# Two levels of attention scores from one product: six groups of queries over the same keys

## The reference, cut to what matters

```python
def step(S, inp):
    qt, kt, vt, gt = inp
    S = S * jnp.exp(gt)[..., None] + kt[..., None] * vt[..., None, :]
    o = jnp.einsum('bhk,bhkv->bhv', qt * scale, S)
    return (S, o)
...
f = 1.0 - k
sign_f = jnp.sign(f4 - 0.5)
theta = jnp.cumsum(sign_f, axis=1) * PI
```

## Time and profile before

| what | value |
|---|---|
| median of 3 runs | 1885.78 us (1882.69 to 1887.09) |
| profiled execution | 1883.84 us, its span 1881.9 us |
| TensorE busy | 1836.1 us, 98% of the span |
| VectorE busy | 1457.9 us, 77% |
| ScalarE busy | 696.8 us, 37% |
| GpSimd busy | 391.4 us, 21% |
| mean granted TensorE clock | 0.994 |
| first score product of block 1 and of block 31 | 107.47 and 1279.06 us |

### The profile page before, as it was taken

The page is one execution under the profiler, slowest core; times in us unless marked ns, Lnnn a source line. Parts: engine busy times, 40 slices in busy tenths (PEclk is TensorE's granted clock), DMA queues, the critical chain, the costliest instruction groups (busy, mean ns, idle before and its releaser), DMA issues. The chain is left out here.

```text
span 1881.9 us, 56458 instructions
## 1 busy us (share of the span) xinstructions
PE 1836.1 (98%) x24873; PEld 1648.7 (88%) x24873; DVE 1457.9 (77%) x2885; ACT 696.8 (37%) x1360; POOL 391.4 (21%) x309
## 2 busy tenths in 40 slices
PE   5899999999999999999999999998999999999999
PEld 5789998999989998899988999887888888888887
DVE  4577777677777777777777777778899889889886
ACT  2243334333343333333333333343334434433433
POOL 1001100111011100111001110012244444344343
PEclk9899999999999999999999999999999999999999
DMA  7010100001000010001100011002111111111110
GB/s 280 3 47 25 47 25 25 24 28 43 25 25 24 33 39 25 24 25 36 35 25 24 25 37 35 24 26 68 60 53 68 68 51 62 68 57 57 68 57 34
DMA packets 42650, 84.88 MB, mean 45 GB/s; under 512 B 2324, under 2 KB 2856, under 8 KB 42408
## 3 DMA queue, kind: packets, MB, share of 16 engines
q1 hardware_dynamic: 38552, 74.46, 11.3%
q10 hardware_dynamic: 3856, 6.82, 1.0%
HBM read 47.72 MB, written 33.55 MB: 43 GB/s over the span
## 5 line engine op out<-in xcount | busy, mean ns | idle before, releaser
L130 POOL TENSOR_TENSOR ln_rs<-ln_ve,mhalf 128x2 f32<-128x2 f32 x64 | 71.2, 1113 | 1011.1 <-DVE ln_ve L125 1011.1
L324 POOL TENSOR_TENSOR xs<-xs,y 128x512 f32<-128x512 f32 x64 | 83.5, 1305 | 368.3 <-DVE y L697 368.3
L1099 PE MATMUL bank<-hT_hi,wq_hi 128*128 128x256 f32 x512 | 152.5, 298 | 4.4 <-DVE wq_lo L1043 4.4
L1099 PE MATMUL bank<-hT_hi,wk_hi 128*128 128x256 f32 x512 | 151.4, 296 | 0.0
L730 DVE TENSOR_TENSOR Tot<-Tot 128x256 f32<-128x256 f32 (+2 forms) x192 | 47.1, 245 | 129.4 <-PE lvl L1176 99.1
L136 DVE TENSOR_SCALAR xn<-xs,ln_mv,ln_rs 128x512 f32<-128x512 f32 x128 | 123.5, 1006 | 29.5 <-POOL ln_rs L130 29.5
L1099 PE MATMUL bank<-hT_lo,wq_hi 128*128 128x256 f32 x512 | 146.3, 286 | 0.0
L1099 PE MATMUL bank<-hT_hi,wq_lo 128*128 128x256 f32 x512 | 145.9, 285 | 0.0
L1099 PE MATMUL bank<-xk_hi,fk_hi 128*128 128x256 f32 x512 | 145.1, 283 | 0.6 <-DVE xk_lo L829 0.6
L1099 PE MATMUL bank<-xk_hi,fk_lo 128*128 128x256 f32 x512 | 144.9, 283 | 0.0
L1099 PE MATMUL bank<-xk_lo,fk_hi 128*128 128x256 f32 x512 | 144.9, 283 | 0.0
(11 more groups left out here) (179 smaller groups left out, 5630.2 us busy)
## 6 DMA issues: line engine op xcount, KB each, us to landing
xs<-in_L_attn_x SPq DMA_DIRECT2D x32, 512.0 KB, 3.6
x_scratch<-xs SPq DMA_DIRECT2D x32, 512.0 KB, 3.2
xs<-x_scratch SPq DMA_DIRECT2D x32, 512.0 KB, 3.5
out<-xs SPq DMA_DIRECT2D x31, 512.0 KB, 2.8
mod_raw<-in_L_wmod SPq DMA_DIRECT2D x4, 1024.0 KB, 15.6
mod_raw<-in_L_wmod ACTq DMA_DIRECT2D x2, 1024.0 KB, 14.2
raw_q<-in_L_attn_wq ACTq DMA_DIRECT2D x1, 1024.0 KB, 12.5
raw_k<-in_L_attn_wk SPq DMA_DIRECT2D x1, 1024.0 KB, 14.3
```

The source lines that it names most:

```text
L130: pool.tensor_tensor(out=ln["rs"][:, :], in0=ln["ve"][:, :], in1=mhalf[:, :], op=ALU.pow).then_inc(ln["rstd"], 1)
L324: pool.tensor_tensor(out=dst, in0=dst, in1=y[:, ch, :], op=ALU.add).then_inc(x2_sb, 1)
L1099: last = pe.matmul(dst, lhs(a, s), rhs(b, s), start=(t == 0), stop=(t == len(terms) - 1))
```

## The change

Levels 2 and 4 are made by one product, and levels 8 and 16 by one (`PAIRS = (2, 8)`). For m = 2 or 8 the tokens stand in quarters of m tokens, four to a segment of 4m. The product takes the keys as they are after level m - the keys of a first quarter reach to its end - and six groups of queries: the quarters 1, 2 and 3 of the queries themselves and three variants in a new buffer `X`: quarter 3 times the decay over quarter 2, quarter 2 times the decay over quarter 1, quarter 3 times the decay over quarters 1 and 2. Six groups are 48 columns. `near_scores` keeps its 48 columns. For all this `Qx` becomes one buffer `QX` of 96 columns per piece: queries of even blocks, odd queries of even and of odd blocks (whose place `X` takes in between), queries of odd blocks.

VectorE gets, for each pair of levels: `neighbours` (a table of products of neighbouring decays), `variants` (3 instructions over 256 elements), `joint` (3 small tables), `pair_update` (3 updates of q and 3 of k over 256 elements each) and `pair_merge` (5 masked copies, of 64 elements, one of 128). These replace, for two levels, 2 tables, 2 updates of q and 2 of k over 512 elements and 2 masked copies of 128. The order in VectorE's body is new: the variance of block n - 1 and its `ogt_low` come after the first variants, `q_odd` comes after the level of 64. On TensorE two products and their waits fall away; the first wide product waits for `x_set` and `level` in the place of level 2, the second stands in the place of level 8. Some raw weights and `h2`, `xk`, `dd` get other addresses, and SyncE's load of SB waits for `mod_cols` 2.

```diff
-LEVELS = [1, 2, 4, 8, 16, 32, 64]  (NL 7, NM 6, NU 7)
+PAIRS = (2, 8)                     (NL 5, NM 10, NU 5)
...
-        Qx = [at(f"Q{n}", [P, G, QB, 48], 114 + 6 * n) for n in range(2)]
-        Q, Qo = [t[:, :, :, 0:32] for t in Qx], [t[:, :, :, 32:48] for t in Qx]
+        QX = at("QX", [P, G, QB, 96], 114)
+        Q, Qo = (QX[:, :, :, 0:32], QX[:, :, :, 64:96]), (QX[:, :, :, 32:48], QX[:, :, :, 48:64])
+        X = QX[:, :, :, 32:64]
...
                 mod_load(CB)
+                sp.wait_ge(mod_cols, 2)
                 mod_load(SB)
...
+                def first_update(n, par):
+                    dve.wait_ge(mm["lvl"], NL * n + 1)
+                    dve.wait_ge(merged, NM * n + 1)
+                    dve.wait_ge(qodd, n + 1)
...
+                def neighbours(n, i):
+                    m = PAIRS[i]
+                    dve.wait_ge(tabs, 9 * n + 4 * i + 1)
+                    t, d = fours(T[m]), fours(D[m])
+                    dve.tensor_tensor(out=d[:, :, 0:3], in0=t[:, :, 0:3], in1=t[:, :, 1:4], op=ALU.mult).then_inc(tabs, 1)
+
+                def variants(n, par, i):
+                    m = PAIRS[i]
+                    t, d, q, x = fours(T[m]), fours(D[m]), quarters(Q[par], m), quarters(X, m)
+                    dve.wait_ge(level, NU * n + i + 1)
+                    dve.tensor_tensor(out=x[:, :, :, 1, :], in0=q[:, :, :, 3, :], in1=spread_over(t[:, :, 2], m), op=ALU.mult)
+                    dve.tensor_tensor(out=x[:, :, :, 2, :], in0=q[:, :, :, 2, :], in1=spread_over(t[:, :, 1], m), op=ALU.mult)
+                    dve.wait_ge(tabs, 9 * n + 4 * i + 2)
+                    dve.tensor_tensor(out=x[:, :, :, 3, :], in0=q[:, :, :, 3, :], in1=spread_over(d[:, :, 1], m), op=ALU.mult
+                                      ).then_inc(x_set, 1)
+
+                def joint(n, i):
...
+                    dve.tensor_tensor(out=d[:, :, 3], in0=d[:, :, 0], in1=t[:, :, 2], op=ALU.mult).then_inc(tabs, 1)
+                    dve.tensor_tensor(out=t[:, :, 1], in0=d[:, :, 1], in1=t[:, :, 3], op=ALU.mult).then_inc(tabs, 1)
+                    dve.tensor_tensor(out=T[4 * m], in0=d[:, :, 0], in1=d[:, :, 2], op=ALU.mult).then_inc(tabs, 1)
+
+                def pair_update(n, par, i):
...
+                    dve.tensor_tensor(out=q[:, :, :, 1, :], in0=q[:, :, :, 1, :], in1=spread_over(t[:, :, 0], m), op=ALU.mult)
+                    dve.tensor_tensor(out=q[:, :, :, 2, :], in0=q[:, :, :, 2, :], in1=spread_over(d[:, :, 0], m), op=ALU.mult)
+                    dve.tensor_tensor(out=q[:, :, :, 3, :], in0=q[:, :, :, 3, :], in1=spread_over(d[:, :, 3], m), op=ALU.mult)
+                    nb = G * P // (4 * m)
+                    for j, u in ((0, t[:, :, 1]), (1, d[:, :, 2]), (2, t[:, :, 3])):
+                        last = dve.tensor_tensor(out=kk[:, :, j, :], in0=kk[:, :, j, :], in1=u.unsqueeze(2).to_broadcast([P, nb, m]),
+                                                 op=ALU.mult)
+                    last.then_inc(level, 1)
...
                 def attention_body(n):            # VectorE
                     par = n % 2
                     diagonal(n, par)
+                    first_update(n, par)
+                    neighbours(n, 0)
+                    first_merge(n, par)
+                    variants(n, par, 0)
+                    joint(n, 0)
                     if n > 0:
                         gated_var(n - 1)
...
+                    neighbours(n, 1)
+                    pair_update(n, par, 0)
+                    variants(n, par, 1)
+                    pair_merge(n, par, 0)
+                    q_silu(n + 1, 1 - par, 0)
+                    joint(n, 1)
+                    q_silu(n + 1, 1 - par, 1)
+                    pair_update(n, par, 1)
+                    pair_merge(n, par, 1)
...
                 def crossing():                   # VectorE
...
+                    pair_update(n, par, 0)
+                    variants(n, par, 1)
+                    pair_merge(n, par, 0)
                     shift(0, "k")
...
+                    joint(n, 1)
                     low(0, "k")
...
+                    pair_update(n, par, 1)
+                    pair_merge(n, par, 1)
...
+                def pair_product(n, par, i):      # TensorE
+                    m = PAIRS[i]
+                    pe.wait_ge(x_set, 2 * n + i + 1)
+                    pe.wait_ge(level, NU * n + i + 1)
...
+                    for g in range(G):
+                        for b in range(QB):
+                            quad = slice(32 * b, 32 * b + 32)
+                            rhs = QX[:, g, b, 32 * par:32 * par + 64].rearrange("p (s four m) -> p s four m", four=4, m=m)[:, :, 1:4, :]
+                            last = pe.matmul(dst[quad, :, g, :], K[par][:, g, quad], rhs, start=True, stop=True)
...
                     rows_of("q", 0, 2, "q")
-                    level_product(n, par, 2)
+                    pair_product(n, par, 0)
                     wait(pe, s_mid, n)
                     rows_of("q", 1, 2, "q")
-                    level_product(n, par, 3)
...
                     rows_of("k", 0, 4, "k")
-                    level_product(n, par, 4)
+                    pair_product(n, par, 1)
                     rows_of("k", 1, 4, "k")
-                    level_product(n, par, 5)
```

More of the change, by code:

```diff
@@ L708, in level_update @@
                 def level_update(n, par, m, idx):
                     nb = G * P // (2 * m)
-                    t = tots(par, m)
+                    t = T[m].rearrange("p (n two) -> p n two", two=2)
                     dve.wait_ge(mm["lvl"], NL * n + idx)
[L712 to L726, removed]
@@ L738, in level_update @@
+                    if m == 32:
+                        dve.wait_ge(tabs, 9 * (n + 1))
+                    dve.tensor_tensor(out=T[2 * m], in0=t[:, :, 0], in1=t[:, :, 1], op=ALU.mult)
+                    c = m // 32
+                    q = Q[par].rearrange("p g (n two c) t -> p g n two c t", two=2, c=c)[:, :, :, 1, :, :]
                     k = K[par][:, :, :].rearrange("p g t -> p (g t)").rearrange("p (n two m) -> p n two m", two=2, m=m)[:, :, 0, :]
@@ L1085, in _ @@
                 dve.wait_ge(mod_set, 3)
+                for i, m in enumerate(PAIRS):
+                    first_half = masks[:, 1 + 2 * i, :].rearrange("p (n two m) -> p n two m", two=2, m=m)[:, :, 0, :]
+                    for j in range(2):
+                        dve.tensor_copy(twice[:, i, :].rearrange("p (n two m) -> p n two m", two=2, m=m)[:, :, j, :], first_half)
                 h_high(1)
@@ L1157, in near_scores @@
                             quad = slice(32 * b, 32 * b + 32)
-                            last = pe.matmul(near(par)[quad, g, :], K[par][:, g, quad], Qx[par][:, g, b, :], start=True, stop=True)
+                            last = pe.matmul(near(par)[quad, g, :], K[par][:, g, quad], QX[:, g, b, 48 * par:48 * par + 48],
+                                             start=True, stop=True)
+                    last.then_inc(mm["lvl"], 1)
+                def pair_product(n, par, i):
+                    m = PAIRS[i]
+                    pe.wait_ge(x_set, 2 * n + i + 1)
+                    pe.wait_ge(level, NU * n + i + 1)
+                    if i == 0:
+                        wait(pe, merged_act, 3 * n)
+                    else:
+                        pe.wait_ge(merged, NM * n + 2)
+                    dst = level_bank(2 + i, par)[:, 0:2 * G * 24].rearrange("p (s g t) -> p s g t", s=2, g=G)
+                    for g in range(G):
[3 more added lines that the diff above has]
+                            last = pe.matmul(dst[quad, :, g, :], K[par][:, g, quad], rhs, start=True, stop=True)
                     last.then_inc(mm["lvl"], 1)
@@ L1162, in level_product @@
                     q, k = Q[par], K[par]
-                    m = LEVELS[idx - 1]
                     pe.wait_ge(level, NU * n + idx - 1)
-                    if idx == 2:
-                        wait(pe, merged_act, 3 * n)
-                    else:
-                        pe.wait_ge(merged, NM * n + idx - 1)
+                    pe.wait_ge(merged, NM * n + (6 if idx == 4 else 10))
                     dst = level_bank(idx, par)
                     for g in range(G):
-                        if m <= 16:
-                            for b in range(QB):
-                                quad = slice(32 * b, 32 * b + 32)
-                                rhs = q[:, g, b, :].rearrange("p (n two m) -> p n two m", two=2, m=m)[:, :, 1, :]
-                                last = pe.matmul(dst[quad, g * 16:g * 16 + 16].rearrange("p (n m) -> p n m", m=m), k[:, g, quad], rhs,
-                                                 start=True, stop=True)
-                        elif m == 32:
+                        if idx == 4:
                             for b in (0, 2):
```

211 lines of the change are left out of this document (120 added, 91 removed).

## The result

The changed kernel takes 1895.87 us (median of 4 runs, 1893.38 to 1896.96), the kernel before 1885.3 in the same session (1882.69 to 1887.09): a ratio of 1.0055, with a 95% interval from 1.0038 to 1.0073. It is slower by 0.55%. The forecast was 1889 us, in a range from 1875 to 1910.

The account below looks back on a forecast made before the run. The prediction took TensorE's own list of work to bound blocks 0 to 30, VectorE the crossing. Block 0 -1.4, blocks 1 to 30 +1 and crossing +4 gave +3.6 on the 1885.78 us median: 1889 us, range 1875 to 1910.

Parts of the forecast that it names:

- The saving per block: TensorE in each block: two wide products replace four narrow ones, 4 x 0.86 - 2 x 1.01 = 1.42 us saved.
- the second rival: TensorE's wide product itself is dearer, through column gaps or a result in two pieces: 1944 us, a quarter 1903; 12%.
- The stall per block: TensorE's second score product waits for VectorE's third variant: start at 6.16 instead of 4.71 us, 1.45 us a block.
- blocks 1 to 30: Ordinary blocks: stall 1.45 less saving 1.42, +0.03 us a block, +1 us in all.
- block 30: The block before the crossing: weight splitting uses up g1_lo's cover ahead of the gate product, 0.1 us.
- The third rival: VectorE's chain: dependent small instructions do not overlap, +0.8 us a block, 1913 us; 3%.
- Block 0: First block: no stall, since modulation products keep TensorE until 75.06, so it gains 1.4 us.
- 0.4 us of cover is left: Ordinary block: g1_lo moves by about 0.6 us and still ends before the gate product, with 0.4 us to spare.
- The crossing: Where attention and feed-forward overlap, VectorE has no room: new work +3.3, uncovered ScalarE cast +0.7; +4 us, 3 to 5.
- The fourth rival: The stall lowers TensorE's clock: 6 us at 0.72 cost about 1.7 us a block, 1940 us; 2%.
- The sum: Whole kernel: -1.4 (block 0) + 1 (blocks 1 to 30) + 4 (crossing) = +3.6 us, forecast 1889 us.

## Why the prediction was right, and where it was off

**The saving per block: right.** 1.42 us forecast, 1.39 in the changed trace and 1.38 with the wait gone. The groups by line show 4096 records of the wide product with a mean like that of the first product's (209 and 208 ns), so neither the missing column group nor the result in two pieces has a price; the second rival falls. VectorE is busy for 3.0 us more in block 14 (32.11 for 29.10), where the prediction has 3.3 in one place and some 4 in another.

```profile
L1265 PE MATMUL lvl<-QX,K 128*32 128x48 f32 x4096 | 57.5, 209 | 48.7 <-DVE QX L749 48.7
```

**The stall per block: right, 0.08 us short.** Forecast was a start at 6.16 us and a stall of 1.45; measured are 6.24 and 1.53. Of the 0.08, 0.06 is the wait between diagonal and level-1 update, 0.09 us where the step allowed 0.03. Small as it is, it was the margin: the forecast difference of 1.45 and 1.42 came out as 1.53 and 1.39, +0.14 a block instead of +0.03, 3.3 of the 4 us by which blocks 1 to 30 exceed the forecast. Most of the rest is of block 1 (0.39 us beyond the others), of block 5 (0.18) and of block 30 (0.19, where the gate product comes 0.16 later than in block 29, behind g_lo; the prediction had 0.1 for it). The third rival, no overlap, falls: 0.60 us from start to start for lengths of 0.69, 0.33 for 0.41 in the rows above.

**Block 0: wrong.** It was to gain 1.4 us and gained nothing; its part of the sum held no wait. TensorE's timeline there:

```profile
99.77 0.50 PE L1189 MATMUL bank<-wg_hi,g_hi 128*128 128x512 f32 x1 [1.82 <-DVE g_lo L694]
```

The gate product waited 0.68 us for g_lo in the kernel before and waits 1.82 now. The prediction named this cover, "0.4 us of cover is left", and used it for ordinary blocks, where it held; in block 0 VectorE has the splitting of weights besides, and the cover was below nothing from the start. g_lo ends when it did (99.71, and 99.64 before), so the products that TensorE saved ahead of it only made it wait there, 1.14 us longer. Another 0.2 is lost sooner: the first wide product starts 19.54 us after the first one where the narrow one started 19.33 after it. This was read from the trace and not tried.

**The crossing: right in kind, too small.** The term was +4 (3 to 5), and +7.0 came. Up to the end of the low part of xk it is +4.9 (18.37 us after the block's first product instead of 13.50), within the step's upper bound of 5: all of the 4.3 summed and the cast, which is waited for by 0.72. From there to the end of the low part of xr it is another 1.7 (27.85 instead of 21.25). About 1.0 of it is the work beside GpSimd, 2.0 us against 1.1 before, a price that the prediction had not in its terms. The other 0.7 is about as long as the second step that releases an addition, which now stands ahead of xr_lo and stood behind it before; this was not tried. A last 0.6 is at the state update. TensorE's products for it (L1306, eight records) start behind a wait of 3.11 us as before, but take 2.04 us where they took 1.45 (the clock granted over them is 0.50 and was 0.72), and VectorE waits 1.84 for them instead of 1.24:

```profile
1326.20 1.12 DVE L862 SCALAR_TENSOR_TENSOR S<-S,TS,bank 128x128 f32<-128x128 f32 x4 [1.84 <-PE bank L1306]
```

Here the lower clock is on the path that VectorE's work follows; why it was lower this time is open. Of the three parts 0.2 comes back by the end. Earlier in the crossing TensorE's windows have a clock of 0.51 behind a wait of 4.32 us, and 0.76 around one of 2.10 (1299.57 to 1306.40). The first of them:

```profile
1290.35:1296.35 6.00, 6.00 (x75) 4.92 (x76) 5.93 (x21) 0.00 (x0) 0.70 (x1) 0.51 0.03 11
```

VectorE is busy for 5.93 of those 6.00 us, so this stretch at a lower clock lies, by this row, off the path that sets the end.

**The fourth rival: not in the changed kernel's ordinary blocks, but near.** 2% was a fair chance only with the wait at 1.46; with 0.46 us more VectorE work it is the main event, 1948 us. Its price was well judged, 1.7 us a block forecast and 1.49 measured. The prediction argued from one 2.19 us wait with a clock of 1.00, and the earlier trace rows could not carry that: 1.92 us of wait repeated in each block lowers the clock in 23 of 30.

**The sum.** -1.4, +1, +4 were to give +3.6; +0.1, +5.0, +7.0 gave +12.1 in the profiled executions. All three terms erred the same way, and the measured median lies 7 us above the forecast. Signs and mechanism hold: the saving is real and the chain ahead of TensorE's second product takes it back.

## What to carry to other kernels

When work is taken from the engine that is full, ask first where in its list the operand of the new step becomes ready: here the product that joins two levels stands where the old one stood, and needs six VectorE instructions more ahead of it. The order that gets the gain is then to make tables in the block before and to let merges wait behind what TensorE waits for: 2.0% faster instead of 0.55% slower, with the same instructions. And a wait on TensorE's path that comes back in each block is to be priced at more than its length once it nears 2 us, since its clock may fall.

## What the runs showed of the hardware

- A wait of 1.92 us in each block lowered TensorE's granted clock in 23 of 30 blocks (1.49 us more each), in a regular order; waits of 1.46 and 1.66 us in nearly every block lowered it in none, and single ones of 2.06 and 2.31 us, in block 1 of two kernels, did not either.
- A product of 32 matmuls (64 records) with 48 columns, in column tiles of 32, runs the same 0.89 us whether the columns lie together or leave out one group of four, and whether its result is written in one piece or two.
- VectorE instructions with two inputs in SBUF lost 1.0 to 1.1 us beside one GpSimd addition (1.67 to 2.69, 1.22 to 2.22, 0.69 to 1.78), predicated copies out of PSUM nothing.
